# Scanning one state of each group from a bank of its own, and adding residual and shared expert by DMA, in a Mamba and MoE kernel

## What is computed

```
xz = layernorm(x) @ in_proj_w.T ; xp, z = halves of 512 channels
xc = silu(causal conv of width 4 over xp)
dt, B, C = split(xc @ x_proj_w.T)            # 64, 16, 16
delta = softplus(dt @ dt_proj_w.T + dt_proj_b)
h[t, e, n] = exp(delta * A[e, n]) * h[t-1, e, n] + delta * xc * B[t, n]     # 512 channels x 16 states
y = sum_n h * C[t, n] + D * xc
x1 = x + (y * silu(z)) @ out_proj_w.T
out = x1 + relu(layernorm(x1) @ Ws1)^2 @ Ws2 + routed experts (with trunc(prob), nearly always 0)
```

## Time and profile before

| | |
|---|---|
| median of 3 runs | 1560.38 us |
| profiled execution, span | 1559.1 us, 1.3 less than the median; its own time has no other figure |
| PE, PEld, DVE, ACT, POOL busy | 1454.6, 1134.1, 1475.8, 1257.4, 1399.0 us |
| scans (line 974) | 1024, 1165.6 us |
| granted TensorE clock, mean | 0.999 |
| DMA | 68 GB/s |

### The profile page before, as it was taken

How to read it: one execution, slowest core, us unless ns; L and a number is a source line. 1 busy time by engine, 2 the same in 40 slices (tenths; PEclk the granted TensorE clock), 3 DMA queues, 4 the chain that set the end, 5 groups by cost and what they waited for, 6 DMA issues and landing times.

```text
span 1559.1 us, 39641 instructions
## 1 busy us (share of the span) xinstructions
PE 1454.6 (93%) x15324; PEld 1134.1 (73%) x15324; DVE 1475.8 (95%) x1775; ACT 1257.4 (81%) x2099; POOL 1399.0 (90%) x1199
## 2 busy tenths in 40 slices
PE   8889999999999999999999999999999999999988
PEld 5666777776777777777777777767777677777777
DVE  6999999999999999999999999999999999998886
ACT  7987887887888888887887888888888887788752
POOL 2899999999999999998999989999998999989994
PEclk9999999999999999999999999999999999999999
DMA  5103031040402305032040301304031040401301
GB/s 161 61 3 136 2 101 66 9 157 3 143 22 65 101 3 164 1 93 73 4 163 3 138 28 47 120 3 164 2 97 69 4 149 3 137 15 43 123 2 56
DMA packets 78512, 106.48 MB, mean 68 GB/s; under 512 B 42289, under 2 KB 67761, under 8 KB 70130
## 3 DMA queue, kind: packets, MB, share of 16 engines
q1 hardware_dynamic: 78322, 103.92, 20.8%
HBM read 86.10 MB, written 17.30 MB: 66 GB/s over the span
## 4 chain that ended last, share of the span: by engine, by line
DVE 32%; PE 20%; ACT 18%; issue 17%; POOL 10%; DMA 1%; SPq 1%; DVEq 1%; ACTq 0%; POOLq 0%
DVE hs L974 29%; PE BX L239 9%; ACT da L638 8%; POOL hs L1271 8%; PE Y L299 3%; PE Y L263 2%; ACT xc L705 1%; DMA cb<-c_scratch 1%; SPq L1406 1%; ACT xp L673 1%; DVE st L986 1%; DVE Y L1005 1%; PE PB L349 1%; ACT x2n L775 1%; POOL rstd L1304 1%
## 5 line engine op out<-in xcount | busy, mean ns | idle before, releaser
L1271 POOL TENSOR_TENSOR hs<-hs,cb 128x1024 f32<-128x1024 f32 x512 | 1210.2, 2364 | 76.3 <-DVE hs L974 55.3
L974 DVE TENSOR_TENSOR_SCAN hs<-da,BX 128x512 f32<-128x512 f32 x1024 | 1165.6, 1201 | 55.5 <-PE BX L239 46.5
L638 ACT ACTIVATE da<-delta,a_neg 128x511 f32<-128x511 f32 (+1 forms) x1024 | 663.6, 711 | 24.9 <-DVE hs L974 24.5
L263 PEld LDWEIGHTS Y<-ident,hs 128*128 128x128 f32 x4096 | 464.5, 141 | 97.3 <-issue 58.0
L263 PE MATMUL Y<-ident,hs 128*128 128x128 f32 x4096 | 510.1, 273 | 14.5 <-POOL hs L1271 14.4
L239 PE MATMUL BX<-bd,uT 32*128 32x128 f32 x8192 | 301.3, 284 | 77.9 <-DVE hs L974 73.8
L239 PEld LDWEIGHTS BX<-bd,uT 32*128 32x128 f32 x8192 | 252.5, 187 | 138.8 <-DVE hs L974 137.7
L299 PE MATMUL Y<-xnT,w_in 128*128 128x512 f32 x240 | 117.6, 613 | 0.7 <-ACT gate L691 0.7
L673 ACT ACTIVATE xp<-Y 128x512 f32<-128x512 f32 x60 | 35.9, 598 | 100.4 <-PE Y L299 99.9
L324 PE MATMUL PA<-w_in,xnT 128*128 128x512 f32 x240 | 114.5, 599 | 0.0
L1005 DVE SCALAR_TENSOR_TENSOR Y<-xp,w_conv,Y 128x512 f32<-128x512 f32 x120 | 88.9, 741 | 3.0 <-ACT Y L675 1.4
(11 more groups left out here) (194 smaller groups left out, 1517.5 us busy)
## 6 DMA issues: line engine op xcount, KB each, us to landing
cb<-c_scratch SPq DMA_DIRECT2D x64, 1024.0 KB, 4.8
x<-in_x SPq DMA_DIRECT2D x16, 512.0 KB, 4.3
x_scratch<-x2T SPq DMA_DIRECT2D x16, 512.0 KB, 6.8
xt<-in_x SPq DMA_DIRECT2D x15, 512.0 KB, 5.3
bd<-bt SPq DMA_DIRECT2D x480, 1.0 KB
out<-x SPq DMA_DIRECT2D x15, 512.0 KB, 3.2
w_in<-in_in_wT SPq DMA_DIRECT2D x1, 1024.0 KB, 8.4
c_scratch<-dbc SPq DMA_DIRECT2D x64, 8.0 KB, 1.5
```

The costliest lines, as they stand in the source:

```text
L263: mm = e.matmul(Y[(G * c + g) % 2][:, t * P:(t + 1) * P], hs[:, k % HR, q, t * P:(t + 1) * P], ident[:, :], is_transpose=True, start=False ...
L638: e.activation(da[:, k % DR, q, h:], delta[:, g, h:], ACT.Exp, scale=a_neg[:, g, n:n + 1]).then_inc(s_da, 1)
L974: e.tensor_tensor_scan(hs[:, k % HR, q, :], da[:, k % DR, q, :], BX[:, :].rearrange("p (t n) -> p n t", n=RT)[:, n % RT, :], float(c % HV) ...
L1271: e.tensor_tensor(hs[:, k % HR, :, :], hs[:, k % HR, :, :], cb[:, Q * p:Q * p + Q, :], ALU.mult).then_inc(s_hc, 1)
```

## The change

1. **A bank for state 15.** The input term of the last state of each group no longer comes from BX. ACT multiplies the transposed u by B's last column into a new tile v (act_v, four products of 128x128 a group, at steps 5, 13, 20 and 29), PE transposes v into PA or PB (the new stage bu, pe_bu, at steps 7, 15, 23 and 31) and VectorE scans state 15 from there. The refill with states 12 to 15 writes three states of four. The next refill waits for 15 scans of the group only. bt is kept twice for this.
2. **Additions by DMA.** ACT copies the output projection into x1 (act_res, steps 11 and 15); POOL issues a DMA that adds x from DRAM to it (pool_add_x, step 15). ACT copies the shared expert's product into x2n (act_shared, steps 2 and 3), and POOL issues a DMA that adds it to the output in DRAM (pool_add_shared, step 3). SP stores x1 at step 20 already, without the shared part. dve_residual and dve_shared go, as does the load sp_xr.
3. **Timetable.** Among others: z of step 30 now stands ahead of dt on PE; the shared products move from PB at step 0 and PA at 2 to PA at 1 and PB at 2; dt of group 2 from PB at 6 to PA at 2; yt of group 2 to step 3; z of step 7 to PB at 6; ut of group 1 to 4; trc to 5 and 6. ACT and VectorE follow, with side work at steps 14, 24 and 28 too.

The diff, cut to its core:

```diff
+BANK_A = {0: [("z", 0, 3)], 1: [("o", -2, 0)], 2: [("dt", 0, 2)], 4: [("yt", -1, 3)], 6: [("trc", 2, 1)], 7: [("bu", 0, 0)],
...
+        def scanned(k):
+            c, i = divmod(k, S)
+            g, p = divmod(i, NP)
+            return released("bu", c, g) if p == NP - 1 else (s_scan, (N - 1) * (G * c + g) + Q * (p + 1))
...
         def pe_bx(e, m):
-            e.wait_ge(s_scan, RT * m)
+            e.wait_ge(s_scan, (N - 1) * (m // NR) + RT * p)
...
+            ns = RT - 1 if p == NR - 1 else RT
...
-                    mm = e.matmul(BX[:, q * CH + j * P:q * CH + (j + 1) * P], uT[rows, g, j, :],
-                                  bd[rows, (NR * c + p) % BR, j, :, :].rearrange("p t n -> p (t n)"), start=True,
+                    mm = e.matmul(BX[:, q * CH + j * P:q * CH + (j + 1) * P].rearrange("p (t n) -> p t n", n=RT)[:, :, 0:ns],
+                                  uT[rows, g, j, :], bd[rows, (NR * c + p) % BR, j, :, 0:ns], start=True,
...
+        def pe_bu(e, c, g):
+            bank, n, done, out = bank_of("bu", c, g)
+            e.wait_ge(out, n)
+            e.wait_ge(s_v, G * c + g + 1)
+            for j in range(J):
+                mm = e.transpose(bank[:, :].rearrange("p (q j t) -> p j q t", q=RT, j=J)[:, j, :, :], v[:, j, :], ident[:, :])
+            mm.then_inc(done, 1)
...
+        def act_v(e, c, g):
...
+            if m:
+                e.wait_ge(*written("bu", *divmod(m - 1, G)))
+            for j in range(J):
+                ins = e.activation(v[:, j, :], uT[:, g, j, :], ACT.Copy, scale=bt[c % 2][:, NR - 1, j, RT - 1:RT])
+            ins.then_inc(s_v, 1)
...
+        def act_res(e, c, kk):
+            bank, n, done, out = bank_of("res", c, kk)
+            e.wait_ge(done, n + 1)
+            e.wait_ge(s_out, 16 * c)
+            e.activation(x1[:, 2 * kk:2 * kk + 2, :], bank[:, :].rearrange("p (t d) -> p t d", t=2), ACT.Copy).then_inc(out, 1)
...
+        def act_shared(e, c, kk):
+            bank, n, done, out = bank_of("o", c, kk)
+            e.wait_ge(done, n + 1)
+            e.activation(x2n[:, 2 * kk:2 * kk + 2, :], bank[:, :].rearrange("p (t d) -> p t d", t=2), ACT.Copy).then_inc(out, 1)
...
-        def dve_scan(e, k):
+        def dve_scan(e, k, q):
...
+            if n == N - 1:
+                bank, use, done, out = bank_of("bu", c, g)
+                e.wait_ge(done, use + 1)
+                e.tensor_tensor_scan(hs[:, k % HR, q, :], da[:, k % DR, q, :], bank[:, :],
+                                     float(c % HV), ALU.mult, ALU.add).then_inc(out, 1)
...
         def dve_stats2(e, c, kk):
-            e.wait_ge(*released("res", c, kk))
+            e.wait_ge(s_res, 16 * (c + 1))
...
+        def pool_add_x(e, c):
+            for kk in range(2):
+                e.wait_ge(*released("res", c, kk))
+            e.dma_start(x1[:, :, :], x_v[c], accum_op=ALU.add).then_inc(s_res, 16)
...
+        def pool_add_shared(e, c):
+            for kk in range(2):
+                e.wait_ge(*released("o", c, kk))
+            e.wait_ge(s_out, 16 * (c + 1))
+            e.dma_start(out_v[c], x2n[:, :, :], accum_op=ALU.add).then_inc(s_acc, 16)
...
+                    if s == 14 and on(c + 1):
+                        dve_tap(e, G * c + 7 if c else G + 3, 2)
...
+                    if s == 24 and on(c + 2):
+                        dve_tap(e, G * c + 8, 0)
...
-                    if s == 4 and on(c - 2):
-                        sp_out(e, c - 2)
-                    if s == 5 and on(c - 1):
-                        sp_xr(e, c - 1)
...
+                    if s == 20 and on(c - 1) and c < NQ - 1:
+                        sp_out(e, c - 1)
```

More of the change, by code:

```diff
@@ L119, in mamba_moe @@
         uT = sb("uT", [P, G, J, P])
-        bt = sb("bt", [P, NR, J, RT])
+        bt = [sb(f"bt{i}", [P, NR, J, RT]) for i in range(2)]
+        v = sb("v", [P, J, P])
         bd = sb("bd", [P, BR, J, KT, RT])
@@ L476, in tensor @@
                     k = S * c + s
[L477 to L480, removed]
                     if s == 16:
@@ L489, in tensor @@
                     if c == 0 and s == 3:
-                        e.wait_ge(s_pa_out, a_use["trc", 1, 1] + 1)
+                        e.wait_ge(s_pb_out, b_use["trc", 1, 0] + 1)
                         for _ in range(8):
-                            e.matmul(PA[:, 0:P], ident[:, :], ident[:, :], start=True, stop=True)
+                            e.matmul(PB[:, 0:P], ident[:, :], ident[:, :], start=True, stop=True)
                     if c and on(c + 1) and s in (4, 12):
@@ L1187, in vector @@
-                    if s == 3 and on(c - 1):
-                        dve_gate(e, c - 1, 3)
-                    if s == 7:
-                        dve_delta(e, c, 2)
+                    dve_scan(e, k, 0)
+                    dve_scan(e, k, 1)
+                    if s == 1:
+                        if c == 0:
+                            dve_tap(e, G, 0)
+                            dve_tap(e, G, 1)
+                        else:
+                            if on(c + 1):
+                                dve_tap(e, G * c + 5, 2)
+                            dve_delta(e, c, 1)
@@ new lines, in vector @@
+                    if s == 3:
+                        if c == 0:
+                            dve_tap(e, G, 2)
+                        if on(c - 1):
+                            dve_gate(e, c - 1, 3)
+                        dve_delta(e, c, 2)
+                    if s == 5 and on(c + 1):
+                        dve_tap(e, G * c + 6 if c else G + 1, 0)
+                        dve_tap(e, G * c + 6 if c else G + 1, 1)
+                    if s == 6 and c == 0:
+                        dve_tap(e, G + 1, 2)
@@ new lines, in vector @@
+                    if s == 9:
+                        if c == 0:
+                            for kk in range(K - 1):
+                                dve_tap(e, G + 2, kk)
+                        else:
+                            if on(c + 1):
+                                dve_tap(e, G * c + 6, 2)
+                            if on(c + 3):
+                                dve_stats(e, c + 3, 0)
+                    if s == 11:
+                        dve_gate(e, c, 0)
+                        if c and on(c + 3):
+                            dve_stats(e, c + 3, 1)
@@ L1222, in vector @@
+                    if s == 27:
+                        dve_gate(e, c, 2)
+                        if on(c - 1):
+                            dve_top(e, c - 1, 0)
+                    if s == 28 and on(c - 1):
+                        dve_top(e, c - 1, 1)
+                    if s == 29 and on(c + 2):
+                        dve_tap(e, G * c + 9, 0)
+                        dve_tap(e, G * c + 9, 1)
             dve_shared_prev(e, 0)
@@ L1430, in sp_out @@
         def sp_out(e, c):
-            for kk in range(2):
-                e.wait_ge(*released("o", c, kk))
+            e.wait_ge(s_res, 16 * (c + 1))
             e.dma_start(out_v[c], x1[:, :, :]).then_inc(s_out, 16)
```

243 lines of the change are left out of this document (104 added, 139 removed), and 6 rows, old and new, of tables (BANK_A, BANK_B).

## The result

The changed kernel takes **1709.24 us** (1706.44 to 1710.64, four runs) against 1560.30 for the kernel before, run beside it: a ratio of 1.095, 95% interval 1.094 to 1.097. It is slower. The forecast was 1675, with a range of 1610 to 1735. The profiled execution has a span of 1707.1 us and took 1708.93.

What follows compares the result with a forecast made beforehand. It took a closed loop of DVE scans and PE refills, with PE waiting for ACT's copies of PA and PB, as the bound: 1559.1 - 35 + 150 = 1674, so 1675 us as a median; range 1610 to 1735.

Steps and rivals of the forecast that it cites:

- DVE alone, -35 us: By VectorE's own work a chunk takes 91.6 us, 2.2 less than before; over 16 chunks -35 us.
- Items 1 to 6: Cycles at steps 30-31, 0-1, 2-3, 6-7, 14-15 and 22-23 each make the next refill late, together 150 us.
- Rival A: ACT is free at each hand-over through PA and PB, so DVE's count decides: 1525 us median; chance 0.08.
- B: Only PE's work counts, no round trips: four-refill cycles late by 2.9 us a chunk, about 1568 us; chance 0.07.
- item 1: Steps 30, 31: z, dt, sum and bu through PA and PB take 7.76 us against 4.74, 3.02 late; 45.3 us.
- C: The refill of three states is slow in PSUM: up to 70 us more, 1745; chance 0.18 together with D.
- D: POOL or the landing of the accumulating DMA bounds: up to 69 us more, 1744; chance 0.18 together with C.
- The products for v: Four 128-column products a group on ACT, taken at 1.2 us a group and costed at nothing as work.

Runs made afterwards that it cites:

- the four orders: Changed kernel, work unchanged: three ACT copies earlier (z at step 30, shared at 2, z of step 1), PE's trc and yt ahead of the sum: 1605.82 us.
- v and dt moved: The four orders, plus dt behind step 29's sum, ht's copy ahead of step 28's exponentials, and v of the fourth group at step 28 on ACT: 1582.43 us.
- the kernel with DVE's additions: Changed kernel with state 15's bank and new timetable kept, but VectorE adding residual and shared expert again, without accumulating DMAs: 1697.77 us, ratio 1.088.
- bu behind the sum: Changed kernel with PE's transposes of bu moved behind the sum of hs products at steps 7, 15, 23 and 31: 1722.56 us, ratio 1.103.
- z first: Changed kernel with only ScalarE's order at step 30 changed, copying z before the softplus of dt: 1727.43 us, ratio 1.106.
- the doubled z: The z first kernel, with PE multiplying z of step 0 twice into PA in chunks 2 to 13: 1710.71 us, ratio 1.095.

## Why the prediction was right, and where it was off

**The mechanism and the sign.** PE's round trips through PA and PB set the time; the waits of the scans for BX and the two banks grew by 171 us, where about 150 was said, and grew at the steps named. The orders alone, with the same work, are worth 103 us (1709 to 1606), and 127 with v and dt moved.

**DVE alone, -35 us.** Right. Chunk time less lateness is 91.4 in the change and in the experiments that leave DVE's list alone, 2.3 below 93.7 (2.2 forecast).

**Items 1 to 6.** Forecast 3.02, 1.73, 2.71, 1.64, 1.02, 0.69; measured 3.14, 1.69, 2.81, 1.78, 1.15, 0.77. Their sum is 11.3 instead of 10.8. One omission: I walked six cycles and took the rest as on time. Steps 5 and 9 are 0.33 and 0.15 late, 0.5 more in a chunk.

**The 33 us that are missing** (a span of 1707.1 against 1674). They lie in these places:

- The twelve chunks 2 to 13 average 103.9 us against 91.6 + 10.8 = 102.4: 18 us. Seven of them take 103.2, and there 1.0 us a chunk is the items and steps 5 and 9, less 0.2 for DVE's pace: 10 us over the twelve. Five take 104.8, and their 1.55 more, 8 us, are the clock.
- Chunk 0 takes 101.0, some 2 more than the forecast's terms give it; chunk 14 101.8, some 3 more.
- The rest, from chunk 15's first scan to the end, takes 123.7 instead of 115.2, where the forecast's terms allow some 117.
- Chunk 1 and what stands ahead of chunk 0 are together 1.5 longer.

Outside chunks 2 to 13 the forecast only counted how often an item occurs, and did not walk them. Step 25 is 0.55 later in every second chunk, where the sum waits for POOL's products (24.6 us in all, 14.4 before), but it costs nothing: step 27 is then on time instead of 0.51 over, and such a chunk, 2 or 4, takes the same 103.2 as chunk 5.

**The clock, a term the forecast left out.** I took the mean granted clock of 0.999 as a given. It is 0.991 now. Chunk 8 shows why: PE after the same 2.84 us wait as in chunk 7, and a window.

```profile
867.16 1.04 PE L282 MATMUL Y<-ident,hs 128*128 128x128 f32 x8
871.04 0.65 PE L384 MATMUL PB<-ident,gate 128*128 128x128 f32 x4 [2.84 <-ACT x2n L811]
871.53 1.48 PE L282 MATMUL Y<-ident,hs 128*128 128x128 f32 x8
872.94 2.09 PE L250 MATMUL BX<-bd,uT 32*128 32x128 f32 x32
```

```profile
872.20:875.40 3.20, 3.20 (x37) 2.65 (x36) 0.30 (x1) 1.34 (x3) 1.76 (x2) 0.50 0.29 28
```

The refill takes 2.09 us instead of 1.17. Steps 3 and 5 together are 1.55 later than in chunk 7, and so they are in chunks 3, 6, 8, 10 and 12 (8 us); in chunk 0 steps 15 and 17 are 1.4 later, and step 3 of chunks 14 and 15 is 1.3 and 1.0 later: some 11 us, a third of what is missing. This fits the 11.5 us by which the kernel with DVE's additions is faster without such stretches. It is larger in the change's neighbours: the clock's records stand at 0.50 for 5 us in the kernel before, 32 in the change, 82 with bu behind the sum and 103 with z first, and half of that time is about what it costs. For z first the doubled z shows that this is why the kernel became slower; for bu behind the sum it is an estimate, 25 us more than in the change, against 13 by which that kernel is slower.

**Rival A** (ACT keeps up) fell with the first waits. **B** (only PE's work) was a lower bound that the reordered kernels approached. Its lateness at steps 31, 7, 15 and 23 was 1.2, 0.8, 0.2 and 0.7; with the four orders 1.30, 0.90, 0.28 and 0.77 were measured, and what that kernel has beyond it is step 1, 1.22, which is ACT's chain, and steps 5, 9 and 21. (B's 1.2 at step 31 counts the sum of step 30 as well, which item 1 leaves out because it runs under the softplus.) 1568 was B's sum, 1582 the best that ran. **C** fell: the refill of three states is no slower. The view by form of PE's line 250 (busy us, mean ns):

```profile
L250 PE MATMUL BX<-bd,uT 32*128 32x128 f32 x6144 | 231.6, 288 | 30.0 <-DVE hs L1031 27.5
L250 PE MATMUL BX<-bd,uT 32*128 32x96 f32 x2048 | 73.4, 278 | 16.8 <-DVE hs L1031 14.9
```

278 against 288 ns, 1.15 against 1.17 us for a whole refill. The Trainium skill (SBUF, State Buffer; the box on cachelines in Door 1) says that a non-contiguous PSUM pattern significantly slows matmuls; here 12 of every 16 bytes are written and no refill is slower, so for this pattern the measurement decides against the sentence. The refill writes a quarter fewer columns in nearly the same time, though, so a smaller penalty per column is not excluded.

**D** fell, but for a remainder. The DMAs' issue on POOL and their landing:

```profile
L1378 POOL DMA_DIRECT2D x<-in_x x15 | 19.8, 1318 | 0.0
```

```profile
x<-in_x POOLq DMA_DIRECT2D x15, 512.0 KB, 6.4
...
out<-x2n POOLq DMA_DIRECT2D x14, 512.0 KB, 6.5
```

6.4 us, below the 6.8 taken from the earlier trace rows, and no DVE wait names them. The Trainium skill's formula (DMA: Bandwidth & Descriptors, Anatomy of one DMA) gives 3.2; the accumulating transfers took twice that here. Plain ones of the same size, issued from SP, took 2.9 (the store out<-x) to 6.7 us (x_scratch<-x2T), so it is not shown that the adding is what doubles it. **The products for v** cost 81.2 us for 64 groups, 1.27 each, where 1.2 was taken; ACT is busy 85.29 us in chunk 7, where 85 was.

## What to carry to other kernels

Where an in-order engine hands a few banks around, walk the chain of every cycle, to the reader's copy and what stands ahead of it, not only the cycles that were edited; put the copy that frees a bank ahead of long work on the reader, and put independent work of the writer between the product and the next use of its bank. A shorter cycle needs less work in it, not only an earlier start. And removing one wait of a closed loop can lengthen the next: the step-30 order alone lost 18 us, the four orders together won 103. A long wait of PE can also cost more than its length, through the granted clock of what follows: look at the clock in the window behind it.
